# Layer norm of a cross-attention kernel: the scaling moved from ScalarE to VectorE one step later, gamma and beta to GpSimd

## The chip, the cores and the metric

The kernel runs on 1 core of one Trainium2 chip. The metric is the device time of one execution in microseconds (us); lower is better. The engines are TensorE (PE, with its weight loads PEld), VectorE (DVE), ScalarE (ACT), GpSimd (POOL) and SyncE (SP), which here only issues DMAs.

## The reference

16 batches of 256 query rows attend to 77 context rows, 16 heads of width 16, model width 256, all float32:

```python
Q, K, V = query @ Wq.T + bq, key_value @ Wk.T + bk, key_value @ Wv.T + bv     # split into 16 heads
attn = softmax(Q @ K.T / sqrt(16))
x = (attn @ V) @ W_o.T + b_o + query
mu, var = mean(x), mean((x - mu) ** 2)                                         # over the 256 columns
out = (x - mu) / sqrt(var + 1e-5) * ln_gamma + ln_beta
```

## The kernel before, in words

Each engine has its own instruction stream, written out by hand, and waits on counting semaphores. After a setup (weights, keys and values of all batches) the work goes in steps `s` = 0 to 18, one batch a step, as a software pipeline. In step `s` the following goes on:

- scores, exponentials and the sums over the context for batch `s`, in five units `u` = 0 to 4 (`UNITS`). For each unit TensorE makes `ps_s`; ScalarE makes `p` and `p_h` from it (lines 785 and 786); GpSimd makes the rest, `p_l = p - p_h` (line 1150). ScalarE may start unit `u` only when GpSimd has done the `p_l` of unit `u - 2`, since `p32` has two buffers. TensorE's `weigh` takes `p_h` and `p_l`.
- the maxima of batch `s + 1`: eight products `max_scores(0)` to `(7)` in two banks `ps_d` on TensorE, and eight reductions `max_of(0)` to `(7)` on VectorE (line 967). Product `j` waits for reduction `j - 2`. ScalarE's `write_maxima` (lines 804 and 805) ends this.
- the output of batch `s - 1`: `denominators` and `normalize` on VectorE (lines 977, 985), `turn_context` on TensorE (line 604), `ctx_h` on ScalarE (line 793, in a step without a query projection behind the exponentials of unit 3), `ctx_l` on VectorE (line 861), `project_out` on TensorE.
- the layer norm of batch `s - 2`: `residual` (line 996), `statistics` (line 1000), `aggregate` (line 1006), and at the end of VectorE's step `centre` (line 1016), (y - mean) * gamma, 128x256 twice. On GpSimd, at the end of its step, `rs_v` and `rs_y` (lines 1165 and 1171), the reciprocal root.
- the store of batch `s - 3`: ScalarE multiplies by the root (line 825, 128x256 twice), GpSimd adds beta (line 1158, 128x512) behind `p_l` of unit 2, SP stores (line 391).

Every even step up to 12 also projects the queries of the next two batches (`project_q`, `query_hi`, `query_lo`), and their DMAs (`load_zero`, `load_twins`, `load_mix`) stand on SP behind the store of the same step, which waits for GpSimd. Every odd step up to 11 ends VectorE's part with `split_x` (`xT_l`, line 861, 128x1024, two SBUF inputs). So the pattern repeats every two steps, about 21.1 us. Below, "odd step" and "even step" are meant in this sense. The last step of VectorE (`s` = 17) does its whole norm in one go, with its end on line 1052. The order of VectorE's step is this list, shortened:

```python
when(S.maxima, (max_of, 2))
...
when(S.maxima, (max_of, 3))
when(S.norm, (statistics, 0))
...
when(S.maxima, (max_of, 4))
...
when(S.output and s < B, (context_lo_part, 0, 1))
when(S.norm, (centre, 0), (centre, 1))
if S.split_x:
```

Of the kernel before, what the change touches and what calls it, by code (L numbers as in the profile page):

```python
# [68 lines left out]
KSLOTS = 4  # L69
PSLOTS = 4  # L70
P32SLOTS = 2
MROWS = 32
WARM_PASSES = 18
LOW_TILES = 3
# [63 lines left out]
def cross_attention_kernel(nc, xT, x, cT, wqT, wkT, wvT, woT, bias_cols, bias_rows, ident,  # L138
                           minus_low, minus_high, out):
    ctx = ExitStack()  # L140
    with ctx:
# [51 lines left out]


        q_mix = [sb("q_mix0", [P, HALVES, 2, PAIR], F32R)]
        result = sb("result", [P, 2, QT, D], F32)
        sb("under_vparts", [P, B * H * VP * VW // 2 - HALVES * 2 * PAIR - 2 * QT * D], F32)
# [4 lines left out]
        ctx_h, ctx_l = sb("ctx_h", [P, HALVES, SQ], F32R), sb("ctx_l", [P, HALVES, SQ], F32R)  # L202
        x_rows = sb("x_rows", [P, 2, QT, D], F32)
        q_mix.append(sb("q_mix1", [P, HALVES, 2, PAIR], F32R))
        y = sb("y", [P, QT, D], F32)


        def bank(name, shape):
# [20 lines left out]
        st_out = [sem(f"st_out{n}") for n in range(2)]  # L229
        st_last = sem("st_last")  # L230

        cleared_k = [sem(f"cleared_k{n}") for n in range(2)]
# [61 lines left out]
        def _(sp):  # L294
# [73 lines left out]
            def step(S):  # L368
                s = S.first
                if S.load_x:  # L370
                    S.wait(sp, x_lo, 1, 4, by=2)
                    sp.dma_start(xT_raw[:], xT_v[:, :, bass.ds(S.lin(SQ, 4 * SQ), PAIR)]).then_inc(ld_xT, 16)
                if S.load_k:
                    if s == 2:
                        sp.wait_ge(k_lo, HALVES * GROUPS)
                    S.wait(sp, pe_s, UNITS, 0)
                    if s <= 4:
                        move_minus((s // 2 + 1) % 2)
                    load_k(S.lin(1, 2), (s // 2 + 1) % 2)
                if S.scores:  # L380
                    if s == 0:
                        sp.wait_ge(pe_v, V_TASKS)
                        sp.wait_ge(pe_bo, 1)
                    S.wait(sp, y_done, 1, -1)
                    sp.dma_start(x_rows[:, s % 2], S.batch(x_v, 0, 0)).then_inc(ld_x[s % 2], 16)
                if s == 0:
                    load_v(1)
                if S.store:
                    if s < LAST_STEP:
                        S.wait(sp, result_done, 1, -2)  # L390
                        sp.dma_start(S.batch(out_v, 3, 0), result[:, (s - 3) % 2]).then_inc(st_out[(s - 3) % 2], 16)
                    else:
                        for t in range(QT):
                            sp.wait_ge(finished, t + 1)
                            sp.dma_start(out_v[B - 1][:, t], result[:, (B - 1) % 2, t]).then_inc(st_last, 16)
# [12 lines left out]
            all_steps(step)  # L408
            sp.wait_ge(st_out[0], 16 * B // 2)
            sp.wait_ge(st_out[1], 16 * (B // 2 - 1))  # L410
            sp.wait_ge(st_last, 16 * QT)


# [285 lines left out]
        def _(act):  # L699
# [73 lines left out]
            def step(S):  # L773
# [34 lines left out]
                for u in range(UNITS):  # L808
# [6 lines left out]
                    if u < HALVES and S.project_q:  # L815
                        S.wait(act, pe_q, 1, 3 + u)
                        S.wait(act, pe_s, UNITS, 0)
                        query_hi(u, (s // 2 + 1) % 2)
                    if u == (2 if S.project_q else 1) and S.store and s < LAST_STEP:

                        S.wait(act, root_done, 1, -2)
                        S.wait(act, centred, QT, -2 * QT)
                        for t in range(QT):
                            r = result[:, (s - 3) % 2, t]
# [31 lines left out]
        def _(dve):  # L856
# [92 lines left out]
            def step(S, between={}):  # L949

                s = S.first
                last = s == B + 1
                own = int(last)
                stats, meanvar = stats_all[:, own], meanvar_all[:, own]
                y_s = x_rows[:, (B - 1) % 2] if last else y[:]
# [34 lines left out]
                def residual():  # L990

                    S.wait(dve, pe_o, 1, -1)
                    S.wait(dve, ld_x[s % 2], 8, -8 * (s % 2))
                    if not last:
                        S.wait(dve, centred, QT, -2 * QT)
# [11 lines left out]

                def centre(t):

                    o = s % 2  # L1010
                    if t == 0:
                        if s == 2:
                            dve.wait_ge(ld_v[1], 16 * NSEG)
                        S.wait(dve, var_done, QT, -QT)
                        S.wait(dve, st_out[o], 8, -16 - 8 * o)
# [20 lines left out]
                if last:  # L1036
# [8 lines left out]
                    dve.wait_ge(var_done, QT * B)  # L1045
                    centre(0)
                    centre(1)
                    dve.wait_ge(centred, QT * B)
                    dve.wait_ge(root_done, B)
                    for t in range(QT):  # L1050
                        r = result[:, (B - 1) % 2, t]
# [59 lines left out]
        def _(pool):  # L1111
# [30 lines left out]
            def step(S):  # L1142
                s = S.first
                for u in range(UNITS):
# [6 lines left out]
                                         ALU.subtract).then_inc(rest16, 1)  # L1151
                    if s == 0 and u in (2, 3):
                        value_low(V_TASKS - 4 + u)
                    if u == (2 if s < B - 1 else 4) and S.store and s < LAST_STEP:

                        r = result[:, (s - 3) % 2]
                        S.wait(pool, scaled, QT, -2 * QT)
                        g_.tensor_tensor(r, r, beta_sb.unsqueeze(1).broadcast_to([P, QT, D]),  # L1158
                                         ALU.add).then_inc(result_done, 1)

                if S.norm:
                    slot = s % 2
                    S.wait(pool, var_done, QT, -QT)
                    S.wait(pool, root_done, 1, -3)
                    g_.tensor_scalar(rs_v[:, slot], meanvar_all[:, int(s == B + 1), :, 1], LN_EPS, 1.0,
                                     ALU.add, ALU.mult).then_inc(eps_added, 1)
                    S.wait(pool, eps_added, 1, -1)
                    S.wait(pool, scaled, QT, -3 * QT)
# [37 lines left out]
```

## Time and profile before

| | |
|---|---|
| median of 3 runs | 213.75 us (213.46 to 214.18) |
| the profiled execution, its own time | 215.56 us |
| its span, first to last instruction | 213.5 us |
| PE, PEld busy | 192.7 us (90%), 173.8 us (81%) |
| DVE busy | 175.5 us (82%) |
| ACT busy | 173.4 us (81%) |
| POOL busy | 152.6 us (71%) |
| mean granted TensorE clock | 0.98 |

Busy time is the sum over an engine's instructions; matmuls overlap, so PE's is not PE at its peak. Four engines lie close together, and no share of busy time tells which one sets the pace of the loop. The chain of work that ended last (each instruction followed back to what released it) and the timeline tell that.

### The profile page before, as it was taken

The page shows a single profiled execution, that of the slowest core. Times are in us where ns is not written, and L with a number is a line of the kernel's source. Part 1 is how long each engine was busy: PE and PEld are TensorE (multiplying, and loading weights), DVE is VectorE, ACT ScalarE, POOL GpSimd, SP SyncE. Part 2 cuts the span into 40 slices and gives each one's busy share as a digit, 9 for nine tenths or more (in the row PEclk, how much of TensorE's full clock was granted, in tenths as well). Part 3 has the DMA queues.
Part 4 walks back from the last instruction along what each step waited for, and adds up shares of the span by engine and source line. Part 5 has one row for each costly group of instructions (what it writes and reads, how often), then busy time and mean ns, then how long its engine had stood idle before and what let it go on. Part 6 is the DMA issues. An engine that isn't in the chain of part 4 may idle for free.

```text
span 213.5 us, 5610 instructions
## 1 busy us (share of the span) xinstructions
PE 192.7 (90%) x2070; PEld 173.8 (81%) x2070; DVE 175.5 (82%) x391; ACT 173.4 (81%) x313; POOL 152.6 (71%) x148
## 2 busy tenths in 40 slices
PE   7898999979999989989998999999999999896830
PEld 4897999869899978977988798879788979795730
DVE  5879985657797898989898989898988997982694
ACT  4588789979888979998999899989998998889130
POOL 9976542596557766896689678867887788979653
PEclk9999999999999999999999999999999999999695
DMA  5945521403656964795479438943793188111112
GB/s 183 350 101 138 146 51 40 163 28 95 204 108 176 240 205 97 186 242 159 86 195 249 136 83 206 244 136 80 187 250 71 53 217 236 54 49 54 49 49 98
DMA packets 32978, 30.39 MB, mean 142 GB/s; under 512 B 11306, under 2 KB 27672, under 8 KB 32952
## 3 DMA queue, kind: packets, MB, share of 16 engines
q1 hardware_dynamic: 31720, 28.78, 51.3%
q10 hardware_dynamic: 1232, 1.26, 2.0%
q8 instruction: 16, 0.26, 0.5%
q14 instruction: 10, 0.08, 0.1%
HBM read 11.32 MB, written 4.19 MB: 73 GB/s over the span
## 4 chain that ended last, share of the span: by engine, by line
PE 29%; POOL 28%; issue 16%; SPq 10%; ACT 6%; DMA 5%; DVE 4%; POOLq 0%; ACTq 0%; DVEq 0%
POOL p_l L1150 18%; PE ps_x L417 14%; PE ps_acc L417 6%; PE ps_s L417 6%; POOL result L1158 5%; SPq L341 4%; POOL rs_y L1171 3%; ACT p_h L786 3%; PE ps_d L417 3%; SPq L302 3%; DMA q_mix<-q_high 3%; DMA w_raw<-in_wkT 2%; DVE result L1016 2%; SPq L319 1%; DVE xT_l L861 1%
## 5 line engine op out<-in xcount | busy, mean ns | idle before, releaser
L1150 POOL TENSOR_TENSOR p_l<-p,p_h 128x512 f16<-128x512 f32 x80 | 95.2, 1195 | 43.2 <-ACT p_h L786 42.3
L967 DVE TENSOR_REDUCE maxima<-ps_d 128x4 f32<-128x308 f32 x128 | 57.3, 466 | 11.2 <-PE ps_d L417 9.4
L785 ACT ACTIVATE p<-ps_s 128x512 f32<-128x512 f32 x80 | 47.5, 594 | 11.2 <-PE ps_s L417 7.1
L786 ACT ACTIVATE p_h<-ps_s 128x512 f16<-128x512 f32 x80 | 47.3, 591 | 0.0
L417 PE MATMUL ps_s<-q_low,kblk 128*128 128x256 f32 x144 | 38.5, 287 | 2.0 <-issue 1.0
L417 PE MATMUL ps_acc<-vblk,p_h 128*128 128x34 f16 (+1 forms) x640 | 32.6, 183 | 0.9 <-POOL p_l L1150 0.9
L417 PEld LDWEIGHTS ps_acc<-vblk,p_h 128*128 128x128 f16 x640 | 28.0, 97 | 5.6 <-issue 1.6
L417 PE MATMUL ps_acc<-vblk,p_l 128*128 128x34 f16 (+1 forms) x320 | 30.5, 182 | 0.0
L417 PEld LDWEIGHTS ps_s<-q_low,kblk 128*128 128x128 f32 x144 | 27.0, 188 | 3.6 <-issue 1.4
L1016 DVE SCALAR_TENSOR_TENSOR result<-y,meanvar,rows_sb 128x256 f32<-128x256 f32 x30 | 28.6, 991 | 0.0
L417 PE MATMUL ps_s<-q_mix,kblk 128*128 128x256 f32 x96 | 26.3, 281 | 0.0
L417 PEld LDWEIGHTS ps_acc<-vblk,p_l 128*128 128x128 f16 x320 | 25.6, 96 | 0.0
L417 PE MATMUL ps_d<-kblk,q_high 128*128 128x308 f32 x64 | 22.0, 349 | 2.7 <-DVE maxima L967 2.6
L417 PE MATMUL ps_s<-q_high,kblk 128*128 128x256 f32 x80 | 23.2, 313 | 0.0
L1158 POOL TENSOR_TENSOR result<-result,rows_sb 128x512 f32<-128x512 f32 x15 | 19.4, 1296 | 3.6 <-ACT result L825 3.6
L417 PE MATMUL ps_d<-kblk,q_low 128*128 128x308 f32 x64 | 20.2, 321 | 1.2 <-ACT q_high L746 0.6
L861 DVE TENSOR_TENSOR ctx_l<-ps_x,ctx_h 128x512 fp32r<-128x512 f32 (+1 forms) x16 | 10.8, 675 | 10.1 <-ACT ctx_h L793 10.1
L417 PE MATMUL ps_x<-wo_h,ctx_l 128*128 128x256 f32 x64 | 18.5, 290 | 0.0
L417 PE MATMUL ps_x<-wo_h,ctx_h 128*128 128x256 f32 x64 | 18.5, 288 | 0.0
L417 PE MATMUL ps_x<-wo_l,ctx_h 128*128 128x256 f32 x64 | 18.4, 288 | 0.0
L417 PEld LDWEIGHTS ps_s<-q_mix,kblk 128*128 128x128 f32 x96 | 18.1, 189 | 0.0
L417 PE MATMUL ps_s<-q_lo,kblk 128*128 128x256 f32 x64 | 18.0, 281 | 0.0
(110 smaller groups left out, 506.1 us busy)
## 6 DMA issues: line engine op xcount, KB each, us to landing
xT_raw<-in_xT SPq DMA_DIRECT2D x8, 512.0 KB, 3.8
x_rows<-in_x SPq DMA_DIRECT2D x16, 256.0 KB, 3.4
out_dram<-result SPq DMA_DIRECT2D x15, 256.0 KB, 2.2
q_mix<-q_lo SPq DMA_DIRECT2D x12, 256.0 KB, 4.7
kblk<-kT SPq DMA_DIRECT2D x64, 38.5 KB, 2.3
kblk<-kblk SPq DMA_DIRECT2D x6, 256.0 KB, 3.3
q_mix<-q_low SPq DMA_DIRECT2D x6, 256.0 KB, 4.4
q_mix<-q_high SPq DMA_DIRECT2D x6, 256.0 KB, 5.1
```

Of the source, the lines that this page charges most:

```text
L302: sp.dma_start(kblk[rows, 2 * slot:2 * slot + 2, :, :, SKV * h:SKV * (h + 1)].rearrange("p b f l k -> p (b f l) k").bitcast(F32), kT[rows, ...
L319: sp.dma_start(q_mix[slot][to, :, part].bitcast(F32), source[slot][rows].bitcast(F32)).then_inc(ld_mix[slot], 16)
L341: sp.dma_start(vblk[part][row:row + n, seg].rearrange("p b f v w -> p (b f v w)"), vparts[part][key:key + n, h].rearrange("p b f v w -> p ...
L417: return nc.tensor.matmul(o, w, m, start=start, stop=stop, skip_group_check=True)
L785: nc.scalar.activation(p32[:, n % P32SLOTS], ps_s[n % 2][:], ACT.Exp, scale=SCALE)
L786: nc.scalar.activation(p_h[:, n % PSLOTS], ps_s[n % 2][:], ACT.Exp, scale=SCALE).then_inc(exp16, 1)
L861: return v_.tensor_tensor(out_, whole, hi.bitcast(F32), ALU.subtract)
L967: v_.tensor_reduce(maxima[:, t, h0:h0 + DMAX_HEADS], ps_d[((DMAX + 1) * (s + 1) + j) % 2][:, 0:DMAX_HEADS * SKV] .rearrange("p (h k) -> p ...
L1016: v_.scalar_tensor_tensor(result[:, o, t], y_s[:, t], meanvar[:, t, 0:1], gamma_sb, ALU.subtract, ALU.mult).then_inc(centred, 1)
L1150: g_.tensor_tensor(p_l[:, n % PSLOTS], p32[:, n % P32SLOTS], p_h[:, n % PSLOTS], ALU.subtract).then_inc(rest16, 1)
L1158: g_.tensor_tensor(r, r, beta_sb.unsqueeze(1).broadcast_to([P, QT, D]), ALU.add).then_inc(result_done, 1)
L1171: g_.tensor_tensor(rs_y[:, slot], rs_v[:, slot], minus_half[:], ALU.pow).then_inc(root_done, 1)
```

## The change

For batches 0 to 13 (`DIRECT`), VectorE computes (y - mean) * root in one `tensor_scalar` with two per-partition scalars, in the step after the statistics, behind `max_of(3)` and ahead of `statistics`. GpSimd then multiplies by gamma behind `p_l` of unit 2, and adds beta behind the same unit in odd steps and behind unit 3 in even steps. ScalarE has no part in it. The store goes out one step later, when its result is already there. `y` and the statistics get two buffers and `result` three. Batches 14 and 15 go as before.

```diff
-        result = sb("result", [P, 2, QT, D], F32)
+        result = sb("result", [P, RSLOTS, QT, D], F32)
-        y = sb("y", [P, QT, D], F32)
+        y_all = sb("y", [P, 2, QT, D], F32)
@@ SP, step
-                    if s < LAST_STEP:
+                    if 0 <= s - 4 < DIRECT:
+                        S.wait(sp, result_done, 1, -3)
+                        sp.dma_start(S.batch(out_v, 4, 0), result[:, (s - 4) % RSLOTS]).then_inc(st_out[(s - 4) % RSLOTS], 16)
+                    if s - 3 == DIRECT:
                         S.wait(sp, result_done, 1, -2)
...
@@ ACT, step
-                    if u == (2 if S.project_q else 1) and S.store and s < LAST_STEP:
+                    if u == (2 if S.project_q else 1) and S.store and DIRECT <= s - 3 < B - 1:
...
@@ DVE, step
+                def normalized():
+                    b = s - 3
+                    if b == 0:
+                        dve.wait_ge(ld_v[1], 16 * NSEG)
+                    S.wait(dve, root_done, 1, -2)
+                    if b >= RSLOTS:
+                        dve.wait_ge(st_out[b % RSLOTS], 16 * (b // RSLOTS))
+                    for t in range(QT):
+                        v_.tensor_scalar(result[:, b % RSLOTS, t], y_all[:, b % 2, t], meanvar_all[:, b % 2, t, 0:1],
+                                         rs_y[:, b % 2, t:t + 1], ALU.subtract, ALU.mult).then_inc(scaled, 1)
...
                 when(S.maxima, (max_of, 3))
+                when(S.store and s - 3 < DIRECT, (normalized,))
                 when(S.norm, (statistics, 0))
...
-                when(S.norm, (centre, 0), (centre, 1))
+                when(s == B, (centre, 0), (centre, 1))
@@ POOL, step
-                    if u == (2 if s < B - 1 else 4) and S.store and s < LAST_STEP:
+                    r = result[:, (s - 3) % RSLOTS]
+                    if u == GAMMA_AT and S.store and s - 3 < DIRECT:
                         S.wait(pool, scaled, QT, -2 * QT)
+                        g_.tensor_tensor(r, r, gamma_sb.unsqueeze(1).broadcast_to([P, QT, D]), ALU.mult).then_inc(gamma_done, 1)
+                    if u == (GAMMA_AT + 1 - s % 2 if s - 3 < DIRECT else 4) and S.store and s < LAST_STEP:
+                        S.wait(pool, scaled, QT, -2 * QT)
+                        if s - 3 < DIRECT:
+                            S.wait(pool, gamma_done, 1, -2)
                         g_.tensor_tensor(r, r, beta_sb.unsqueeze(1).broadcast_to([P, QT, D]),
                                          ALU.add).then_inc(result_done, 1)
```

## Rows read from the trace of the kernel before

**Rows 1.** One pair of steps: window, length, busy PE, PEld, DVE, ACT, POOL, clock, DMA.
```profile
111.04:132.13 21.09, 20.08 (x234) 17.90 (x233) 19.14 (x44) 19.30 (x36) 16.21 (x18) 1.00 0.66 167
```

**Rows 2.** The chain that ended last, 126 to 141 us: start, us, what.
```profile
126.48 1.25 POOL result L1158
127.73 1.31 POOL p_l L1150
129.04 0.84 issue
...
131.45 0.71 POOL rs_y L1171
132.16 2.26 POOL p_l L1150 x2
...
137.14 1.39 DVE result L1016
138.53 1.15 DVE xT_l L861
139.72 1.66 PE ps_x L417 x6
```

**Rows 3.** Timeline of VectorE in the same odd step.
```profile
132.22 0.74 DVE L1000 BATCH_NORM_STATS2 stats<-y 128x6 f32<-128x256 f32 x2
...
133.03 0.44 DVE L967 TENSOR_REDUCE maxima<-ps_d 128x4 f32<-128x308 f32 x1
...
136.70 1.83 DVE L1016 SCALAR_TENSOR_TENSOR result<-y,meanvar,rows_sb 128x256 f32<-128x256 f32 x2
```

**Rows 4.** Timeline of TensorE there: product 6 of the maxima, last score of unit 3.
```profile
133.53 0.41 PE L417 MATMUL ps_d<-kblk,q_high 128*128 128x308 f32 x1 [0.43 <-DVE maxima L967]
...
134.01 0.28 PE L417 MATMUL ps_s<-q_low,kblk 128*128 128x256 f32 x1
```

**Rows 5.** Timeline of ScalarE there: exponentials of unit 3.
```profile
134.49 0.60 ACT L785 ACTIVATE p<-ps_s 128x512 f32<-128x512 f32 x1
```

**Rows 6.** Timeline of GpSimd there: units 0 to 2, and unit 3.
```profile
132.12 3.57 POOL L1150 TENSOR_TENSOR p_l<-p,p_h 128x512 f16<-128x512 f32 x3
...
136.90 1.35 POOL L1150 TENSOR_TENSOR p_l<-p,p_h 128x512 f16<-128x512 f32 x1
```

**Rows 7.** Timeline of VectorE in the even step that follows.
```profile
144.56 0.26 DVE L977 RECIPROCAL recip<-ps_acc 128x16 f32<-128x16 f32 x1 [0.63 <-PE ps_acc L417]
```

**Rows 8.** By line: min/median/max ns of one centring and one `p_l`.
```profile
L1016 DVE SCALAR_TENSOR_TENSOR result<-y,meanvar,rows_sb x30: 472/981/1475, 62.6 to 205.7; 128x256 f32<-128x256 f32 x30
L1150 POOL TENSOR_TENSOR p_l<-p,p_h x80: 1155/1167/1362, 36.2 to 197.9; 128x512 f16<-128x512 f32 x80
```

**Rows 9.** Groups of instructions: busy us, mean ns of one, idle before.
```profile
L1158 POOL TENSOR_TENSOR result<-result,rows_sb 128x512 f32<-128x512 f32 x15 | 19.4, 1296 | 3.6 <-ACT result L825 3.6
L825 ACT ACTIVATE result<-result,rs_y 128x256 f32<-128x256 f32 x30 | 13.6, 507 | 2.6 <-POOL rs_y L1171 2.6
L1093 DVE CAST bo_parts<-rows_sb 128x256 fp32r<-128x256 f32 x1 | 0.3, 297 | 0.0
```

**Rows 10.** Timeline of VectorE in the setup: two casts.
```profile
16.80 1.69 DVE L922 CAST kblk<-vblk 32x768 fp32r<-32x768 f32 x1
18.51 1.24 DVE L923 CAST kblk<-vblk 32x464 fp32r<-32x464 f32 x1
```

**Rows 11.** Timeline of GpSimd in the setup, beside them.
```profile
16.27 1.80 POOL L1134 MEMSET vblk<- 128x2040 uint32 x1
18.19 1.31 POOL L1125 TENSOR_TENSOR vparts<-vwhole,vparts 77x512 f16<-77x512 f32 x1
```

**Rows 12.** Waits in SP's queue: who for whom, us in total, times, longest.
```profile
SPq L391 <- POOL result L1158: 45.8, 15, 9.0
```

**Rows 13.** Waits of the compute engines, 44 to 90 us.
```profile
PE ps_s L417 <- DMA q_mix<-q_high: 0.7, 1, 0.7
```

**Rows 14.** Timeline of GpSimd in step 16: beta of batch 13.
```profile
204.19 1.28 POOL L1158 TENSOR_TENSOR result<-result,rows_sb 128x512 f32<-128x512 f32 x1 [2.62 <-ACT result L825]
```

More of the change, by code:

```diff
@@ L71 @@
 P32SLOTS = 2
+RSLOTS = 3
+GAMMA_AT = 2
+DIRECT = B - 2
 MROWS = 32
@@ L195, in cross_attention_kernel @@
         q_mix = [sb("q_mix0", [P, HALVES, 2, PAIR], F32R)]
-        result = sb("result", [P, 2, QT, D], F32)
-        sb("under_vparts", [P, B * H * VP * VW // 2 - HALVES * 2 * PAIR - 2 * QT * D], F32)
+        result = sb("result", [P, RSLOTS, QT, D], F32)
+        sb("under_vparts", [P, max(1, B * H * VP * VW // 2 - HALVES * 2 * PAIR - RSLOTS * QT * D)], F32)
         p32 = sb("p32", [P, P32SLOTS, 2, SQ], F32)
@@ L228, in cross_attention_kernel @@
         ld_x = [sem(f"ld_x{n}") for n in range(2)]
-        st_out = [sem(f"st_out{n}") for n in range(2)]
+        st_out = [sem(f"st_out{n}") for n in range(RSLOTS)]
+        gamma_done = sem("gamma_done")
         st_last = sem("st_last")
@@ L388, in step @@
                 if S.store:
-                    if s < LAST_STEP:
+                    if 0 <= s - 4 < DIRECT:
+                        S.wait(sp, result_done, 1, -3)
+                        sp.dma_start(S.batch(out_v, 4, 0), result[:, (s - 4) % RSLOTS]).then_inc(st_out[(s - 4) % RSLOTS], 16)
+                    if s - 3 == DIRECT:
                         S.wait(sp, result_done, 1, -2)
-                        sp.dma_start(S.batch(out_v, 3, 0), result[:, (s - 3) % 2]).then_inc(st_out[(s - 3) % 2], 16)
-                    else:
+                        sp.dma_start(S.batch(out_v, 3, 0), result[:, (s - 3) % RSLOTS]).then_inc(st_out[(s - 3) % RSLOTS], 16)
+                    if s == LAST_STEP:
                         for t in range(QT):
                             sp.wait_ge(finished, t + 1)
-                            sp.dma_start(out_v[B - 1][:, t], result[:, (B - 1) % 2, t]).then_inc(st_last, 16)
+                            sp.dma_start(out_v[B - 1][:, t], result[:, (B - 1) % RSLOTS, t]).then_inc(st_last, 16)
                 if S.project_q and s >= 2:
@@ L408, in _ @@
             all_steps(step)
-            sp.wait_ge(st_out[0], 16 * B // 2)
-            sp.wait_ge(st_out[1], 16 * (B // 2 - 1))
+            for n in range(RSLOTS):
+                sp.wait_ge(st_out[n], 16 * len(range(n, B - 1, RSLOTS)))
             sp.wait_ge(st_last, 16 * QT)
@@ L818, in step @@
                         query_hi(u, (s // 2 + 1) % 2)
-                    if u == (2 if S.project_q else 1) and S.store and s < LAST_STEP:
+                    if u == (2 if S.project_q else 1) and S.store and DIRECT <= s - 3 < B - 1:
                         S.wait(act, root_done, 1, -2)
-                        S.wait(act, centred, QT, -2 * QT)
+                        act.wait_ge(centred, QT)
                         for t in range(QT):
-                            r = result[:, (s - 3) % 2, t]
+                            r = result[:, (s - 3) % RSLOTS, t]
                             nc.scalar.activation(r, r, copy, scale=rs_y[:, (s - 3) % 2, t:t + 1]).then_inc(scaled, 1)
@@ L952, in step @@
                 last = s == B + 1
-                own = int(last)
+                own = s % 2
                 stats, meanvar = stats_all[:, own], meanvar_all[:, own]
-                y_s = x_rows[:, (B - 1) % 2] if last else y[:]
+                y_s = x_rows[:, (B - 1) % 2] if last else y_all[:, own]
                 def accumulated(f):
@@ L994, in residual @@
                     if not last:
-                        S.wait(dve, centred, QT, -2 * QT)
+                        S.wait(dve, scaled, QT, -3 * QT)
                     v_.tensor_tensor(y_s.rearrange("p t d -> p (t d)"), ps_x[1][:],
@@ L1008, in centre @@
                 def centre(t):
-                    o = s % 2
+                    o = (s - 2) % RSLOTS
                     if t == 0:
-                        if s == 2:
-                            dve.wait_ge(ld_v[1], 16 * NSEG)
                         S.wait(dve, var_done, QT, -QT)
-                        S.wait(dve, st_out[o], 8, -16 - 8 * o)
+                        dve.wait_ge(st_out[o], 16 * ((s - 2) // RSLOTS))
                     v_.scalar_tensor_tensor(result[:, o, t], y_s[:, t], meanvar[:, t, 0:1], gamma_sb,
                                             ALU.subtract, ALU.mult).then_inc(centred, 1)
+                def normalized():
[8 more added lines that the diff above has]
+                                         rs_y[:, b % 2, t:t + 1], ALU.subtract, ALU.mult).then_inc(scaled, 1)
                 def context_lo_part(*halves):
@@ L1047, in step @@
                     centre(1)
-                    dve.wait_ge(centred, QT * B)
+                    dve.wait_ge(centred, 2 * QT)
                     dve.wait_ge(root_done, B)
                     for t in range(QT):
-                        r = result[:, (B - 1) % 2, t]
+                        r = result[:, (B - 1) % RSLOTS, t]
                         v_.scalar_tensor_tensor(r, r, rs_y[:, (B - 1) % 2, t:t + 1], beta_sb, ALU.mult, ALU.add).then_inc(finished, 1)
@@ L1164, in step @@
                     S.wait(pool, root_done, 1, -3)
-                    g_.tensor_scalar(rs_v[:, slot], meanvar_all[:, int(s == B + 1), :, 1], LN_EPS, 1.0,
+                    g_.tensor_scalar(rs_v[:, slot], meanvar_all[:, slot, :, 1], LN_EPS, 1.0,
                                      ALU.add, ALU.mult).then_inc(eps_added, 1)
```

1 line of the change is left out of this document (removed).

## The prediction

> **What bounds the kernel now.** I read the windows of one pair of steps first, then the chain that ended last, then each engine's timeline around it. The windows [rows 1] show a pair of 21.09 us in which VectorE works 19.14, ScalarE 19.30 and GpSimd 16.21, at a granted clock of 1.00 (its full 2.4 GHz). No engine is full, so the pace is set by a ring of waits. The reader is to see in the chain [rows 2] that it goes through GpSimd from unit 2 of the even step (whose `p_l` ends at 126.48) to unit 1 of the odd one, with one gap of 0.84 us, then through ScalarE's exponentials and `ctx_h`, through `ctx_l` and the two centrings on VectorE, `xT_l`, and TensorE's query projection.
>
> The chain hides how close VectorE is behind it. In the odd step VectorE's `max_of(4)` starts at 133.03 [rows 3]; TensorE's product 6 starts at 133.53 and stood idle 0.43 us for it; the last score of unit 3 comes behind that product, at 134.01 for 0.28, so it ends at 134.29 [rows 4]. ScalarE starts the exponentials of unit 3 at 134.49 [rows 5], which waited for `p_l` of unit 1, done at 134.42 (132.16 + 2.26) [rows 2]. So the middle of VectorE's odd step has some 0.2 us of slack, no more. What is put ahead of `max_of(4)` beyond that delays unit 3, then `ctx_h`, which stands behind unit 3 on ScalarE, then `ctx_l`, `project_out` and the next step. In the even step there is more: VectorE waits 0.63 us for TensorE just ahead of `max_of(4)` [rows 7].
>
> **Where VectorE and GpSimd get in each other's way.** One centring takes 472 ns at best, 981 in the median and 1475 at worst [rows 8]. The pair at 136.70 shows why: it lasts 1.83 us, beside beta until about 136.9 and `p_l` of unit 3, which starts at 136.90 and takes 1.35 in place of 1.17 [rows 3, 6, 8]. The first centring gets through as beta ends and holds up `p_l` by 0.18; the second waits until `p_l` ends at 138.25 and is itself over at 138.53. A centring reads two tensors, but a cast, which reads one, does the same: the cast of 768 elements from 16.80 ends at 18.49, 0.42 after GpSimd's memset (18.07); that of 464 elements from 18.51 ends at 19.75, 0.25 after GpSimd's subtraction (19.50) [rows 10, 11]. Undisturbed a cast of 256 elements takes 297 ns [rows 9]. The two waiting casts differ by 0.17 us for 304 elements, so one of 256 would end about 0.25 - 208 x 0.17 / 304 = 0.13 us after GpSimd lets it in.
>
> **The change part by part.**
>
> Removed from VectorE: the pair of centrings, 2 x 0.98 us a step [rows 8]. In odd steps it is on the chain, ahead of `xT_l`. But TensorE is only just behind there: its projection starts at 139.72 as `xT_l` ends at 139.68 (138.53 + 1.15) [rows 2], and it works 20.08 of 21.09 us [rows 1]; that is worth at most 0.3 us a pair by TensorE's idle share, and I take nothing, since `ctx_l` and `project_out` remain.
>
> Removed from ScalarE: 2 x 0.51 us a step [rows 9]. In the odd step ScalarE waits for GpSimd anyway. In the even step it would let unit 4 come earlier and close GpSimd's gap of 0.84 us [rows 2], but GpSimd fills it itself:
>
> Added to GpSimd: gamma, an operation of beta's form, 1.25 us on the chain [rows 2] (1.30 at most [rows 9]). In the even step: from 126.48, gamma 1.25, `p_l` of unit 3 in 1.17 (its 1.31 less the wait for a centring), beta 1.25: unit 4 starts at 130.15, where it was 129.88 (129.04 + 0.84). That is 0.25 us later, and all that follows up to unit 1 of the odd step with it. In the odd step gamma and beta stand between units 2 and 3, where the next reader of a unit is the following step; GpSimd has 4.88 us idle a pair (21.09 - 16.21) [rows 1] against 2.5 added, so I cost it at nothing. Were that cover gone it would be 1.25 us a pair.
>
> Added to VectorE's middle: two `tensor_scalar` of 256 elements. The trace has none of this size. From below: as the cast, 0.30 us each, overlapping like their neighbours to 0.45 for two [rows 9]. From above, if each waits for a whole `p_l` of 1.17: 2 x (1.17 + 0.13) = 2.6. I take waiting, since the row nearest to it in form, the cast, waits. In the odd step VectorE comes to the pair at 132.22, GpSimd starts unit 0 at 132.12 and works without a gap to 135.65 [rows 3, 6]. And the pair must itself wait for `rs_y`, which ended at 132.16 and will end at 132.41, when GpSimd's next `p_l` is ready to go. Two outcomes:
> - GpSimd goes first: both wait. Unit 0 ends at 132.12 + 0.25 + 1.17 = 133.54, the first is over 0.13 later, unit 1 takes until 134.85, the second is over at about 134.95. Statistics and `max_of(4)` come 2.7 us late (134.95 - 132.22); less the slack of 0.2 the step is 2.5 us longer.
> - VectorE goes first: only the second waits, until 133.75. 1.5 late, 1.3 us longer.
>
> The Trainium skill, "SBUF — State Buffer", section "Who interferes with whom", says that a VectorE instruction in a 2-port mode, with `tensor_scalar` named among them, and a GpSimd instruction exclude each other for a whole instruction. The casts agree (0.42 and 0.25 us after GpSimd's end); no row shows it for `tensor_scalar`.
>
> In the even step the pair finds GpSimd in the gap between units 0 and 1 once the odd step has grown, and its 0.5 us fit into the 0.63 idle [rows 7]: nothing.
>
> Moved store: SP issues it one step later, when its result is there. SP's 45.8 us of waits for GpSimd go [rows 12], and the six DMAs of even steps behind them start sooner. A compute engine waited for these once, 0.7 us [rows 13]: a gain of 0.7 at most, at step 4, taken as nothing since the longer step 3 covers that wait.
>
> The end: in step 16 beta (1.28) starts at 204.19 upon ScalarE's pair [rows 14]; now gamma comes ahead of it, 1.28 more, less some 0.3 by which VectorE's pair is shorter than ScalarE's (1.01 against 0.5 to 0.7). All that follows is one series through GpSimd: +1.0 us. Step 14, without a query projection, meets the same row of `p_l`, partly covered: +0.7 (0.4). Step 15 reduces no maxima: nothing.
>
> **The sum**, over odd steps 5 to 13 (five), step 3 with its 0.7 us of waiting for a DMA and a later start on GpSimd, step 14, and the end. Both wait: 5 x 2.5 + 0.8 + 0.7 + 1.0 = 15.0. One waits: 5 x 1.3 + 0.5 + 0.4 + 1.0 = 8.4. The profiled execution took 215.56 us (span 213.5 and 2.06 around it), 0.8% over the median of the runs, 213.75. To that median the two give 215.56 + 15.0 = 230.6, x 213.75 / 215.56 = 228.6, and 222.1. Who goes first hangs on less than 0.1 us, which the trace doesn't settle; I take the middle, 225.5.
>
> **The rivals.**
> - No waiting (218 us). `tensor_scalar` takes turns with nothing, like the statistics. For it: the two statistics take 0.74 us together beside `p_l` and aren't stretched [rows 3, 6]. Against it: the casts. The pair then costs 0.25 for the later `rs_y` and 0.6 for itself, less 0.2 of slack: 5 x 0.65 + 0.4 + 1.0 = 4.6 us, 218.3. The Trainium skill (same page and section) has this rule too: one SBUF input outside the 2-port modes doesn't contend.
> - GpSimd alone (216 us). VectorE's time is won back elsewhere in the step and only 0.25 a pair and the end remain: 6 x 0.25 + 1.0 = 2.5.
> - Faster (212 us). The pair runs in no more than the 0.2 us of slack beyond what it frees, and from there the lost centrings decide: TensorE's projection comes up to 0.3 us earlier in six pairs, and the DMA wait of 0.7 goes: -2.5, +1.0 at the end: about -1.5. For it: VectorE loses 1.96 us a step and ScalarE 1.01. Against it: they are lost at the end of the step, and the new work stands ahead of `max_of(4)`, for which TensorE waits already.
>
> **How the numbers follow.** Waiting 0.68, no waiting 0.14, GpSimd alone 0.06 (half a per cent and more over before), faster 0.08, and 0.04 for gains and losses that cancel. A measurement tells about 0.3% from no change. Faster 0.09, same 0.05, slower 0.86. The time is that of the waiting pair, 225.5, its own range 221 to 230; down to 217 the range takes in no waiting: 217 to 230.5.
>
> **What would show it.** `tensor_scalar` well above 0.3 us in odd steps (1.2 to 1.4 for the waiting one) and near 0.3 in even steps; `p_l` of units 0 and 1 stretched by about 0.1; product 6 waiting 1.5 to 3 us for `max_of(4)` in odd steps; a pair of 22.4 to 23.6 us; idle time of GpSimd moved ahead of unit 3 of odd steps; SP no longer waiting for GpSimd. The prediction is wrong if `tensor_scalar` takes 0.3 to 0.4 us beside `p_l`, or if product 6 waits no longer than before.

## The result: 235.7 us, 9.8% slower

The changed kernel takes 235.66 us (median of 6 runs, 233.86 to 236.47) against 214.03 (213.46 to 215.33) for the kernel before in the same job: a ratio of 1.098, with a 95% interval of 1.095 to 1.102. The forecast was 225.5, with a range of 217 to 230.5: the direction was right, the size was not. The profiled execution took 236.47 us with a span of 234.7, so 21.2 us more than the span before.

**The pair of steps.** The windows of after, one pair of steps (it answers to [rows 1]) and the stretch behind TensorE's wait in its odd step (length, busy PE, PEld, DVE, ACT, POOL, clock, DMA):

```profile
138.20:162.11 23.91, 20.93 (x234) 19.06 (x234) 18.68 (x44) 17.78 (x32) 18.24 (x19) 0.93 0.58 150
141.90:146.30 4.40, 4.39 (x53) 4.23 (x54) 2.96 (x8) 2.83 (x5) 3.50 (x3) 0.64 0.11 34
```

The pair has grown from 21.09 to 23.91 us, by 2.8. VectorE and ScalarE do less work in it than before (18.68 and 17.78 against 19.14 and 19.30). GpSimd does more, and TensorE is busy for longer (20.93 against 20.08) with the same 234 matmuls, part of them at a lower clock. And the granted clock of a pair, 1.00 before, is 0.93: over the 4.4 us behind product 6 it is 0.64, a mean between the two levels of 1.2 and 2.4 GHz.

The odd step on VectorE (it answers to [rows 3]), and the pair in the even step that follows:

```profile
138.32 2.36 DVE L1033 TENSOR_SCALAR result<-y,meanvar,rs_y 128x256 f32<-128x256 f32 x2
140.60 0.74 DVE L1007 BATCH_NORM_STATS2 stats<-y 128x6 f32<-128x256 f32 x2
141.26 0.23 DVE L984 RECIPROCAL recip<-ps_acc 128x16 f32<-128x16 f32 x1
141.42 0.43 DVE L974 TENSOR_REDUCE maxima<-ps_d 128x4 f32<-128x308 f32 x1
...
151.28 0.95 DVE L1033 TENSOR_SCALAR result<-y,meanvar,rs_y 128x256 f32<-128x256 f32 x2
```

GpSimd beside it (it answers to [rows 6]):

```profile
137.53 0.70 POOL L1193 TENSOR_TENSOR rs_y<-rs_v,minus_half 128x2 f32<-128x2 f32 x1
138.20 3.56 POOL L1168 TENSOR_TENSOR p_l<-p,p_h 128x512 f16<-128x512 f32 x3
141.72 1.27 POOL L1175 TENSOR_TENSOR result<-result,rows_sb 128x512 f32<-128x512 f32 x1
...
150.59 1.17 POOL L1168 TENSOR_TENSOR p_l<-p,p_h 128x512 f16<-128x512 f32 x1
```

The last line is unit 0 of the even step. In the kernel before, the same one is this:

```profile
141.72 1.17 POOL L1150 TENSOR_TENSOR p_l<-p,p_h 128x512 f16<-128x512 f32 x1
```

From unit 0 to unit 0, the odd step has grown from 9.60 us (141.72 - 132.12) to 12.39 (150.59 - 138.20). The even step has not: 11.52 us (162.11 - 150.59) against 11.50 (153.22 - 141.72). So the whole loss of a pair of steps arises in its odd step.

The pair of `tensor_scalar` begins 0.12 us behind GpSimd's unit 0 and lasts as long as two `p_l`. GpSimd's three `p_l` take 3.56 us, as before (3.57): it loses nothing, VectorE does all the waiting. `max_of(4)` comes 3.22 us behind unit 0 (141.42 - 138.20) instead of 0.91 (133.03 - 132.12).

By line, one of the new instructions on VectorE, min/median/max ns:

```profile
L1033 DVE TENSOR_SCALAR result<-y,meanvar,rs_y x28: 400/976/1256, 68.2 to 223.3; 128x256 f32<-128x256 f32 x28
```

The shortest, 400 ns, is the undisturbed one (in run 6 below, where GpSimd stands still beside most of them, the median is 406); the longest is that plus most of a `p_l`.

TensorE's product 6 and the scores behind it, at the lower clock (it answers to [rows 4]: 0.43 us of idle time, 0.41 for the product, 0.28 for a score):

```profile
141.91 0.62 PE L424 MATMUL ps_d<-kblk,q_high 128*128 128x308 f32 x1 [2.72 <-DVE maxima L974]
142.33 0.41 PE L424 MATMUL ps_s<-q_low,kblk 128*128 128x256 f32 x1
```

ScalarE's exponentials of unit 3 (to [rows 5]) now wait for TensorE:

```profile
143.21 0.60 ACT L792 ACTIVATE p<-ps_s 128x512 f32<-128x512 f32 x1 [2.67 <-PE ps_s L424]
```

**The clock.** The page's row of TensorE's granted clock in 40 slices, after:

```profile
PEclk9999999999999999799979997999799979896785
```

A slice is 5.9 us. The five 7s ahead of the last six slices are the odd steps 5 to 13. Before, the row holds nothing below 9 until the last three slices. Here the clock fell behind an idle stretch of TensorE of 2.7 us; behind the 0.43 us of before it did not.

**SP.** Waits in its queue, after (to [rows 12]: 45.8 us, 15 times):

```profile
SPq L395 <- POOL result L1180: 16.4, 2, 9.4
```

Both waits are behind 186 us: the stores no longer wait inside the loop, as the change means them to. TensorE had waited once, for 0.7 us, for a DMA behind them [rows 13], so there was next to nothing to win; run 7 below shows no gain.

**Where the 21.2 us of span arise.** By the starts of GpSimd's unit 0 in both kernels: up to step 13, +11.7 (186.00 against 174.31); step 13, +3.6 (12.38 us for 8.77); step 14, +2.7 (12.23 for 9.56); step 15 to the end, +3.2 (24.1 for 20.9). The last three together are 9.5 us, nearly half of the loss, behind the start of step 13.

### The profile page after: what moved, and what is told of

Its sections match the earlier page's. It is cut to its first block, busy times and chain, and to the rows that moved or that the text cites. A ratio compares the mean times of both kernels' runs of the same rounds, so it can differ in the third digit from the quotient of the medians.

```text
span 234.7 us, 5596 instructions
## 1 busy us (share of the span) xinstructions
PE 197.2 (84%) x2070; PEld 179.4 (76%) x2070; DVE 175.0 (75%) x391; ACT 162.8 (69%) x285; POOL 169.2 (72%) x162
## 4 chain that ended last, share of the span: by engine, by line
PE 39%; POOL 20%; DVE 17%; issue 12%; SPq 7%; ACT 2%; DMA 1%; POOLq 0%; DVEq 0%; ACTq 0%
PE ps_x L424 14%; PE ps_s L424 8%; PE ps_acc L424 8%; POOL p_l L1168 6%; DVE result L1033 5%; PE ps_d L424 5%; DVE maxima L974 5%; SPq L345 4%; PE ps_x L611 3%; POOL vparts L1143 3%; DVE stats L1007 3%; SPq L306 2%; POOL result L1175 2%; POOL kblk L1133 2%; POOL result L1180 2%
## 5 line engine op out<-in xcount | busy, mean ns | idle before, releaser
L1168 POOL TENSOR_TENSOR p_l<-p,p_h 128x512 f16<-128x512 f32 x80 | 93.1, 1169 | 48.3 <-ACT p_h L793 47.5
L424 PE MATMUL ps_s<-q_low,kblk 128*128 128x256 f32 x144 | 39.2, 291 | 1.4 <-issue 1.2
L424 PE MATMUL ps_d<-kblk,q_high 128*128 128x308 f32 x64 | 24.4, 386 | 18.3 <-DVE maxima L974 17.8
L424 PE MATMUL ps_acc<-vblk,p_h 128*128 128x34 f16 (+1 forms) x640 | 34.3, 187 | 0.3 <-issue 0.3
L424 PEld LDWEIGHTS ps_acc<-vblk,p_h 128*128 128x128 f16 x640 | 29.9, 100 | 5.1 <-issue 1.8
L424 PE MATMUL ps_acc<-vblk,p_l 128*128 128x34 f16 (+1 forms) x320 | 31.9, 186 | 0.0
L424 PEld LDWEIGHTS ps_s<-q_low,kblk 128*128 128x128 f32 x144 | 28.5, 198 | 2.0 <-issue 1.3
L424 PEld LDWEIGHTS ps_d<-kblk,q_high 128*128 128x128 f32 x64 | 13.2, 209 | 20.8 <-DVE maxima L974 20.8
L424 PEld LDWEIGHTS ps_acc<-vblk,p_l 128*128 128x128 f16 x320 | 27.0, 99 | 0.0
L1033 DVE TENSOR_SCALAR result<-y,meanvar,rs_y 128x256 f32<-128x256 f32 x28 | 23.3, 872 | 1.8 <-POOL rs_y L1193 1.8
L424 PE MATMUL ps_s<-q_high,kblk 128*128 128x256 f32 x80 | 24.1, 323 | 0.0
L1180 POOL TENSOR_TENSOR result<-result,rows_sb 128x512 f32<-128x512 f32 x15 | 19.6, 1304 | 2.2 <-ACT result L832 1.0
L1175 POOL TENSOR_TENSOR result<-result,rows_sb 128x512 f32<-128x512 f32 x14 | 17.9, 1278 | 2.9 <-DVE result L1033 2.9
```

Of the source, the lines that this page charges most:

```text
L424: return nc.tensor.matmul(o, w, m, start=start, stop=stop, skip_group_check=True)
L1033: v_.tensor_scalar(result[:, b % RSLOTS, t], y_all[:, b % 2, t], meanvar_all[:, b % 2, t, 0:1], rs_y[:, b % 2, t:t + 1], ALU.subtract, ALU ...
L1168: g_.tensor_tensor(p_l[:, n % PSLOTS], p32[:, n % P32SLOTS], p_h[:, n % PSLOTS], ALU.subtract).then_inc(rest16, 1)
L1175: g_.tensor_tensor(r, r, gamma_sb.unsqueeze(1).broadcast_to([P, QT, D]), ALU.mult).then_inc(gamma_done, 1)
```

## The experiments

The theory: two `tensor_scalar` in the middle of VectorE's odd step wait for two whole `p_l`; TensorE's product 6 waits for them; TensorE's clock then falls. The rivals put the loss down to gamma on GpSimd, to the place of the pair, or to the end of the kernel.

**1. The pair on its own.** The kernel before, with two more `tensor_scalar` into a scratch tile behind `max_of(3)`, and nothing else of the change.

```diff
+                def extra():
+                    S.wait(dve, root_done, 1, -2)
+                    for t in range(QT):
+                        v_.tensor_scalar(scratch[:, t], gamma_sb, meanvar_all[:, 0, t, 0:1],
+                                         rs_y[:, (s - 3) % 2, t:t + 1], ALU.subtract, ALU.mult)
...
                 when(S.maxima, (max_of, 3))
+                when(S.store and s - 3 < B - 2, (extra,))
```

> The kernel before, with nothing but two tensor_scalar of 128x256 added (gamma's row into a tile that nobody reads) behind max_of(3), in the steps and after the wait of the change. Theory (the pair at this place is the cost): the pair takes 2.2 to 2.5 us in odd steps, the clock falls behind it, 230 to 238 us. Rival (the costs come from gamma on GpSimd, the store or the buffers): 214 to 218 us.

Measured: 236.07 us (ratio 1.100, 1.093 to 1.107). The pair in an odd step on VectorE:

```profile
139.69 2.23 DVE L1023 TENSOR_SCALAR scratch<-rows_sb,meanvar,rs_y 128x256 f32<-128x256 f32 x2
```

TensorE's product 6 behind it:

```profile
143.15 0.62 PE L418 MATMUL ps_d<-kblk,q_high 128*128 128x308 f32 x1 [2.59 <-DVE maxima L968]
```

These two instructions a step cost as much as the whole change, with centrings, ScalarE, gamma, beta and stores all as before. That is enough to make the loss.

**2. One instruction instead of two.** The same, with `for t in range(1)`.

> The kernel before with one added tensor_scalar behind max_of(3) instead of two (two took 236.1 us). Theory (each waits for one whole p_l): it takes 1.1 to 1.2 us in odd steps, max_of(4) is some 1.1 us late and the kernel takes 220 to 225 us. Rival (the wait comes once for the pair, whatever their number): 230 us or more.

Measured: 217.43 us (1.012, 1.008 to 1.017), and cheaper than either text expected. One pair of steps, windows:

```profile
132.66:154.28 21.62, 19.79 (x233) 17.92 (x233) 20.30 (x46) 19.27 (x36) 15.99 (x17) 1.00 0.66 161
```

Its odd step on VectorE:

```profile
132.84 1.14 DVE L1023 TENSOR_SCALAR scratch<-rows_sb,meanvar,rs_y 128x256 f32<-128x256 f32 x1
...
137.62 0.69 DVE L862 TENSOR_TENSOR ctx_l<-ps_x,ctx_h 128x512 fp32r<-128x512 f32 x1 [0.55 <-ACT ctx_h L794]
138.23 1.05 DVE L1017 SCALAR_TENSOR_TENSOR result<-y,meanvar,rows_sb 128x256 f32<-128x256 f32 x2
139.21 1.22 DVE L862 TENSOR_TENSOR xT_l<-xT_raw,xT_h 128x1024 fp32r<-128x1024 f32 x1
```

TensorE there:

```profile
135.21 0.41 PE L418 MATMUL ps_d<-kblk,q_high 128*128 128x308 f32 x1 [1.50 <-DVE maxima L968]
```

GpSimd there:

```profile
137.44 1.16 POOL L1158 TENSOR_TENSOR p_l<-p,p_h 128x512 f16<-128x512 f32 x1
```

`ctx_l` and `xT_l` of the kernel before, to compare:

```profile
136.09 0.69 DVE L861 TENSOR_TENSOR ctx_l<-ps_x,ctx_h 128x512 fp32r<-128x512 f32 x1 [0.71 <-ACT ctx_h L793]
...
138.45 1.21 DVE L861 TENSOR_TENSOR xT_l<-xT_raw,xT_h 128x1024 fp32r<-128x1024 f32 x1
```

The `tensor_scalar` does wait for one `p_l`, and product 6 comes 1.07 us later (1.50 - 0.43). But the pair of steps is only 0.53 us longer, and the clock stays at 1.00. Counted from unit 0 (132.66 here, 132.12 before), `ctx_l` starts 0.99 later (4.96 us against 3.97) and `xT_l` only 0.22 (6.55 against 6.33). The `p_l` of unit 3 has not moved: it starts 4.78 us behind unit 0 in both (137.44 - 132.66, and 136.90 - 132.12 [rows 6]). The centrings, 0.99 later, now meet only its last 0.37 us, and take 1.05 us in place of the 1.83 of [rows 3]. So the first wait costs about 3 us in all and the second nearly 19. Waiting time does not add up in a straight line here.

**3. TensorE kept busy in its wait.** The changed kernel, with 16 matmuls that nobody reads ahead of product 6, in the steps without a query projection.

```diff
+                        if j == 6 and s >= 3 and not S.project_q:
+                            S.wait(pe, ctx_lo, 1, -1)
+                            for _ in range(16):
+                                mm(ps_x[0][:, 0:SQ], warm_rows[:, 0:P], warm_rows[:], True, True)
                         S.wait(pe, max_done, DMAX, DMAX + j - 1)
```

> The changed kernel, with 16 matmuls on zeros (about 1.8 us) on TensorE ahead of product 6 in steps without a query projection, where it waits 2.7 us; their output is overwritten unread. Theory (the fall of the clock after the wait is part of the cost, about 0.8 us in a pair): clock 0.97 or more, 229 to 232 us. Rival (the clock costs nothing, it falls where TensorE waits anyway): 235 us as without them.

Measured: 230.03 us (1.075, 1.068 to 1.082), inside the theory's 229 to 232. TensorE, odd step:

```profile
137.40 1.92 PE L424 MATMUL ps_x<-warm_rows 128*128 128x256 bf16 x16
140.09 0.41 PE L424 MATMUL ps_d<-kblk,q_high 128*128 128x308 f32 x1 [0.78 <-DVE maxima L978]
```

One pair of steps, windows:

```profile
136.41:159.39 22.98, 21.58 (x252) 19.38 (x249) 18.89 (x44) 17.73 (x32) 18.28 (x20) 1.00 0.58 151
```

Product 6 comes as late as before the filling (1.92 + 0.78 = 2.70), but now runs in 0.41 us, and the clock is 1.00. The pair is 22.98 us, 0.93 less than after. So of the 2.8 us a pair some 1.9 is waiting and 0.9 is clock. Over the kernel the clock is 5.6 us by the medians (235.66 - 230.03), 7.1 by the two profiled spans.

**4. A form of the instruction that does not wait.** The changed kernel, its `tensor_scalar` also writing out an accumulator, its place unchanged.

```diff
-                                         rs_y[:, b % 2, t:t + 1], ALU.subtract, ALU.mult).then_inc(scaled, 1)
+                                         rs_y[:, b % 2, t:t + 1], ALU.subtract, ALU.mult, accum_out=acc_sb[:, t:t + 1]).then_inc(scaled, 1)
```

> The changed kernel, with an accumulator output on the two tensor_scalar, at the same place; the output need not be the layer norm. If only a form that can use a second port waits for GpSimd, this one takes 0.40 to 0.50 us each at any time, and the kernel takes 217 to 221 us. If every VectorE instruction on SBUF of this kind waits, 2.3 us for the pair in odd steps and 235 us remain.

Measured: 220.8 us (1.031, 1.025 to 1.036), in the theory's range. The line's two instructions, min/median/max ns:

```profile
L1034 DVE TENSOR_SCALAR_CACHE_REDUCE result<-y,meanvar,rs_y x28: 527/530/537, 68.4 to 208.0; 128x256 f32<-128x256 f32 x28
L1034 DVE DVE_READ_ACCUMULATOR result<-y,meanvar,rs_y x28: 77/81/85, 68.8 to 208.5; 128x1 f32 x28
```

All 28 take the same 530 ns, in odd and even steps, beside the same three `p_l`: slower by itself than the 400 ns of the plain form, yet 15 us cheaper. (With the accumulator the output is no longer the layer norm, so this version is a measurement and not a remedy.) The Trainium skill, "SBUF — State Buffer", section "Who interferes with whom", names `tensor_scalar` among the operations that can hold the port pair that VectorE and GpSimd share, and excepts the form that writes out its accumulator. This run agrees: 530 ns at every meeting, against up to 1256.

What is left, 6.7 us over the kernel before, is of the size of run 2: the two instructions and their reads of the accumulator still take about 1.1 us ahead of `max_of(4)`, product 6 waits 1.36 us for it, and a pair of steps takes 21.61 us (155.25 - 133.64, by unit 0), 0.52 over before. Of the 6.1 us of span, 2.6 arise up to step 13 and 3.5 behind it.

**5. Gamma left out.** The changed kernel without the multiplication by gamma on GpSimd (and without the wait for it in front of beta).

```diff
-                        g_.tensor_tensor(r, r, gamma_sb.unsqueeze(1).broadcast_to([P, QT, D]), ALU.mult).then_inc(gamma_done, 1)
+                        pass
```

> The changed kernel without GpSimd's multiplication by gamma, which is left out. Theory: 232 to 235 us, since GpSimd has room in the longer pair and only the end of the kernel gains about 1.3 us. Rival (GpSimd's load is what costs): 217 to 222 us.

Measured: 234.67 us (1.096, 1.090 to 1.102). That is 1.0 us below the changed kernel, which lies within the two intervals: in this order of the work gamma costs next to nothing. The prediction had priced it at 2.5 us in all.

**6. The pair late in odd steps.** The changed kernel, with the pair ahead of `ctx_l` in odd steps and in step 14, and behind `max_of(3)` in even steps as it was.

```diff
-                when(S.store and s - 3 < DIRECT, (normalized,))
+                late = s % 2 == 1 or s == B - 2
+                when(S.store and s - 3 < DIRECT and not late, (normalized,))
...
+                when(S.store and s - 3 < DIRECT and late, (normalized,))
                 when(S.output and s < B, (context_lo_part, 0, 1))
```

> The changed kernel, with VectorE's pair of tensor_scalar moved from behind max_of(3) to ahead of ctx_l in odd steps and in step 14. There GpSimd has to wait for the pair, so nothing holds it up. Theory (the pair waits for two p_l ahead of max_of(4), and TensorE's wait lets its clock fall): the pair takes 0.5 to 1.2 us there, product 6 waits no longer than before, the clock is back at 0.97 or more, 216 to 219 us. Rival (GpSimd's added gamma is what costs): 230 us or more.

Measured: 235.02 us (1.098, 1.090 to 1.105). The theory's 216 to 219 missed by 16 us. VectorE, from the pair of an odd step to that of the next, even step:

```profile
144.57 0.73 DVE L1033 TENSOR_SCALAR result<-y,meanvar,rs_y 128x256 f32<-128x256 f32 x2
...
146.14 1.60 DVE L868 TENSOR_TENSOR xT_l<-xT_raw,xT_h 128x1024 fp32r<-128x1024 f32 x1 [0.25 <-ACT xT_h L756]
...
152.24 2.55 DVE L1033 TENSOR_SCALAR result<-y,meanvar,rs_y 128x256 f32<-128x256 f32 x2 [1.01 <-POOL rs_y L1195]
```

GpSimd beside it:

```profile
145.38 1.29 POOL L1177 TENSOR_TENSOR result<-result,rows_sb 128x512 f32<-128x512 f32 x1 [0.68 <-DVE result L1033]
146.81 2.08 POOL L1182 TENSOR_TENSOR result<-result,rows_sb 128x512 f32<-128x512 f32 x1
148.85 2.29 POOL L1170 TENSOR_TENSOR p_l<-p,p_h 128x512 f16<-128x512 f32 x2
...
151.50 0.70 POOL L1195 TENSOR_TENSOR rs_y<-rs_v,minus_half 128x2 f32<-128x2 f32 x1
152.17 2.47 POOL L1170 TENSOR_TENSOR p_l<-p,p_h 128x512 f16<-128x512 f32 x2
```

The odd step is cured: the pair takes 0.73, because GpSimd stands still, waiting for it. But gamma then starts late, beta meets `xT_l` and takes 2.08 in place of 1.28, and the reciprocal root comes only at 152.2. The pair of the even step waits 1.01 us for it, starts as GpSimd starts the next two `p_l`, and waits for both (2.55 us). The same loss has moved one step on: product 6 of even steps now waits 2.8 us.

**7. The same without gamma.** Run 6 with gamma left out as in run 5.

> The kernel with the pair late in odd steps and in step 14 only (the one that took 235 us), without GpSimd's multiplication by gamma, which is left out. Theory (there GpSimd, with gamma, beta and the wait for the pair in a row, makes rs_y late, so that the pair of the even step waits for rs_y and then for two p_l): without gamma rs_y is 1.3 us earlier, the pair of even steps takes 1.3 us or less, 217 to 222 us. Rival (the even step loses by its place alone): 230 us or more.

Measured: 214.47 us (0.9997, 0.996 to 1.003), the time of the kernel before, and better than the expectation. Gamma is worth 20.6 us between runs 6 and 7 and 1.0 us between the changed kernel and run 5: what an operation costs depends on whether the root behind it is awaited. In run 7 the pair of the even step waits for no root and takes 1.43 us (the theory said 1.3 or less). The run also shows that all the rest of the change together (the pair in a good place, ScalarE's and the centrings' work gone, the store a step later, the buffers) comes to nothing that can be told from the noise; it does not show that each part does.

**8. The pair late in every step up to 15.** Run 6 with `late = s < B`, gamma kept.

> The changed kernel with the pair of tensor_scalar ahead of ctx_l in every step up to 15, even steps too. Theory (what costs is VectorE waiting for p_l ahead of max_of(4), in whichever step the pair stands there): product 6 waits 0.5 us at most in both steps, the clock is 0.97 or more, 217 to 222 us, with 0.3 to 0.5 us lost per even step where the pair delays ctx_l. Rival (GpSimd can't carry gamma as well, wherever the pair stands): 228 us or more.

Measured: 222.4 us (1.037, 1.031 to 1.042), just above the theory's range, and the best time of any version that does the whole change and computes the layer norm. One pair of steps, windows:

```profile
134.13:156.07 21.94, 20.21 (x234) 17.97 (x233) 17.93 (x45) 17.48 (x32) 19.05 (x19) 1.00 0.63 157
```

TensorE's product 6 in the odd step:

```profile
135.09 0.41 PE L424 MATMUL ps_d<-kblk,q_high 128*128 128x308 f32 x1 [0.27 <-DVE maxima L974]
```

The clock is full, and product 6 waits only 0.27 us in the odd step and 0.22 in the even one. GpSimd is busy 19.05 of 21.94 us and waits 0.55 us for the pair in each step. That this is what costs the remaining 8 us was not tested.

**9. Centrings behind `xT_l`.** The kernel before, with only the order of these two on VectorE swapped in odd steps, to see what taking the centrings off that place is worth.

```diff
-                when(S.norm, (centre, 0), (centre, 1))
                 if S.split_x:
                     S.wait(dve, x_hi, 1, 5, by=2)
                     split_x()
+                when(S.norm, (centre, 0), (centre, 1))
```

> The kernel before, with VectorE's xT_l ahead of the two centrings in odd steps instead of behind them. Theory (the centrings are on the chain, but TensorE is less than 0.3 us behind): xT_l ends 1 to 1.8 us earlier and 0 to 0.3 us a pair is gained, 212.0 to 214.2 us. Rival (xT_l now holds up a p_l of GpSimd): 214.5 to 217 us.

Measured: 217.19 us (1.011, 1.007 to 1.016): a loss. VectorE in the odd step:

```profile
116.28 2.11 DVE L861 TENSOR_TENSOR xT_l<-xT_raw,xT_h 128x1024 fp32r<-128x1024 f32 x1 [0.25 <-ACT xT_h L749]
118.32 1.81 DVE L1016 SCALAR_TENSOR_TENSOR result<-y,meanvar,rows_sb 128x256 f32<-128x256 f32 x2
```

GpSimd beside it, units 3 and 4:

```profile
116.13 1.18 POOL L1150 TENSOR_TENSOR p_l<-p,p_h 128x512 f16<-128x512 f32 x1
118.67 1.17 POOL L1150 TENSOR_TENSOR p_l<-p,p_h 128x512 f16<-128x512 f32 x1 [1.36 <-ACT p_h L786]
```

`xT_l` takes up the wait for `p_l` of unit 3 in the centrings' stead (2.11 for 1.15). The centrings still follow, and meet the `p_l` of unit 4 (1.81).

**10. The end.** Three versions of the changed kernel, in which the new way ends with batch 9, 11 and 12 (`DIRECT` smaller, the old way for the rest).

```diff
-DIRECT = B - 2
+DIRECT = B - 6
...
-                when(s == B, (centre, 0), (centre, 1))
+                when(S.norm and s - 2 >= DIRECT, (centre, 0), (centre, 1))
```

(`B - 4` and `B - 3` in the other two.)

> The changed kernel with the new way for batches 0 to 9 only, and 10 to 15 in the old way (centring, ScalarE, beta), so that steps 13 to 16 have no pair behind max_of(3). If the end of the kernel costs what the two traces show (6 to 7 us from step 13 on): 228 to 231 us. If it costs 1.7 to 2.5 us as forecast: 233 to 235 us.

> The changed kernel with the new way for batches 0 to 11 only; 12 to 15 go the old way, so steps 15 and 16 have no pair and no gamma. Theory (step 15 costs too: its pair waits beside the three p_l like the others, the only chain of the end goes through it, and TensorE's clock falls further behind it; step 16 adds 1.0): by the traces step 15 to the end took 24.1 us against 20.9 before, so about 232.5 us (231.5 to 233.3). Rival (the forecast's step: step 15 nothing, the end 1.0): 234.6, no different from the version that goes the new way up to batch 12.

> The changed kernel with the new way for batches 0 to 12, so only step 16 has no pair and no gamma. Theory and the forecast agree here: gamma ahead of beta in the last series through GpSimd costs about 1.0 us, so 234.6 us (234.2 to 235.0). Rival (step 16 is worth nothing or far more, since the idle stretches of the end move with the clock): 235.6, or below 233.5.

Measured: 227.19 us (1.058, 1.050 to 1.065), 232.86 (1.087, 1.081 to 1.092) and 234.84 (1.098, 1.091 to 1.104). Windows of the first, from unit 0 of step 13 to the end:

```profile
186.73:225.60 38.87, 26.41 (x323) 23.71 (x321) 27.69 (x67) 22.72 (x46) 28.64 (x31) 0.89 0.26 80
```

That stretch is 39.2 us in the kernel before (213.5 - 174.31) and 48.7 after (234.7 - 186.00), so with the old way (38.9) it is as before. Steps 13 to 16 cost 8.5 us of the 21.6, a little more than the theory's 228 to 231 allowed. Taken apart by the medians: step 16 costs 0.8 (235.66 - 234.84), step 15 2.0 (234.84 - 232.86), steps 13 and 14 the other 5.7. The versions ran in different jobs; by their ratios to the kernel before, times 214.03, the three are 0.2, 2.3 and 6.2. The intervals of the last two versions overlap a little, so the cost of step 15 is right in sign and rough in size, and that of step 16 lies within the noise. Why step 15 costs something, VectorE after, in step 15:

```profile
210.74 2.34 DVE L1033 TENSOR_SCALAR result<-y,meanvar,rs_y 128x256 f32<-128x256 f32 x2 [1.79 <-POOL rs_y L1193]
213.00 0.74 DVE L1007 BATCH_NORM_STATS2 stats<-y 128x6 f32<-128x256 f32 x2
...
213.94 0.48 DVE L992 SCALAR_TENSOR_TENSOR ctx_n<-ps_acc,v_unscale,recip 128x256 f32<-128x256 f32 x1
```

The chain that ended last, after, at the same place:

```profile
211.84 1.24 DVE result L1033
213.08 0.66 DVE stats L1007 x2
...
214.02 0.41 DVE ctx_n L992
...
214.47 1.11 PE ps_x L611 x4
```

`ctx_n` of the same step in the kernel before, where unit 0 starts at 192.64:

```profile
192.47 0.48 DVE L985 SCALAR_TENSOR_TENSOR ctx_n<-ps_acc,v_unscale,recip 128x256 f32<-128x256 f32 x1
```

No maxima are reduced in step 15, but `ctx_n` stands behind the pair on VectorE too, and TensorE's `turn_context` behind that. The pair first waits 1.79 us for the root and then for two `p_l`, so `ctx_n` starts 3.33 us behind unit 0 (213.94 - 210.61), where it started 0.17 ahead of it before. `turn_context` then runs at the lower clock (1.11 us for four, at 0.50; 0.60 at the full one in an odd step of run 3). Before, the chain ran through GpSimd here and VectorE had room.

## Why the prediction was wrong, step by step

- **What bounds the kernel; the slack ahead of `max_of(4)`.** Right. The loss came through `max_of(4)`, product 6 and unit 3, as put. Lateness is not passed on in full, though: 1.07 us at product 6 cost 0.53 a pair in run 2.
- **`tensor_scalar` waits for `p_l`.** Right: 976 ns in the median, 400 at least; the "no waiting" rival fell in runs 1 and 4. The lower bound read off the cast, 0.30 us, was too low: 0.40. "`p_l` stretched by 0.1" did not come: 3.56 us for three.
- **Who goes first: the middle of two outcomes.** This step failed first. The prediction said that the order hangs on less than 0.1 us, which the trace does not settle, and took the mean of 228.6 and 222.1. GpSimd goes first in each of the odd steps 5 to 13, as at 138.20 and 138.32 above. Rows 3 and 6 already had the order, 132.12 and 132.22. The prediction made a tie of it, by leaving VectorE's arrival at 132.22 and letting both engines wait for a root that comes 0.25 us later. In the trace after, VectorE waits for no root: it goes from `max_of(3)` to the pair without idle time and is 0.12 us behind GpSimd (0.30 in step 5), where it was 0.10 before. The likeliest outcome was "both wait". A mean of two outcomes is a time that neither gives.
- **"Both wait", 2.5 us an odd step.** Up to step 13 this came out as 10.8, and measured 11.7, but for mixed reasons. The waiting alone is 1.9 a pair (run 3), less than the 2.5; TensorE's clock adds 0.9, which no term of the sum held. Had only the order been right, 228.6 would have stood near run 3's 230.0, the time with the clock held for most of the kernel; but that nearness would be luck. In run 3 the loss is 8.1 us up to step 13 and 6.0 behind it (in spans), where "both wait" has 10.8 and 4.2: one term too dear, the other too cheap. The term that was missing altogether, the clock, is 5.6 us.
- **The even step: nothing.** Right for the change: 11.52 us against 11.50. The pair does not quite fit the gap, though. It starts at 151.28, beside the `p_l` of unit 0 (until 151.76), and takes 0.95 us. Wrong as a general rule: in run 6 it is the even step that pays.
- **Gamma on GpSimd: 0.25 a pair, +1.0 at the end.** Too dear, if anything: 1.0 us in all by run 5, and 0.2 to 0.8 for step 16 by the last version of run 10, both within the noise. The warning beside it, what it costs if its cover goes, was too low: 20.6 us between runs 6 and 7, not 1.25 a pair.
- **The end: step 14 0.7, step 15 nothing.** This failed too. Step 13, priced as one more odd step at 2.5, is 3.6 longer (2.3 with the clock held). Step 14 is 2.7 longer, and 1.5 with the clock held (run 3: 11.08 for 9.56); the cover it was granted, "partly covered", was a guess. Step 15 costs 2.0 to 2.3. It was costed by the one reader, `max_of(4)`, that is missing there, and not by who else stands behind the pair on VectorE.
- **Removed work on VectorE and ScalarE, and the store: nothing.** Right: run 7 has all of it, and the time of the kernel before. Run 9 shows why for the centrings: what they cost is largely the meeting with `p_l`, and the next instruction takes that over.

The sum as it should have been, in spans: 11.7 up to step 13, 3.6, 2.7 and 3.2. Of it, 7.1 is clock by the two profiled spans (that of after is of the slowest of its six executions), and 5.6 by the medians. What stays open: run 3's filling leaves step 15 and the end without a filled wait, so the clock's whole share there was not separated; why 0.3 of the 0.53 us of run 2 arises behind `xT_l` was not followed; and what costs the last 8 us of run 8 is argued, not shown.

## What to carry to other kernels

Before an operation is put into a gap, look not only at how busy its engine is but at what the neighbour that shares its access does at that moment: two instructions of 400 ns took 2.4 us here beside GpSimd and 0.7 where GpSimd itself was waiting for it. When two outcomes hang on a small difference, take one, by the order that the rows already show, and give the other its chance. And when a wait of TensorE grows from tenths of a microsecond to some 2.7 us, price the clock behind it as well: here it was another half of the waiting.

## What the runs showed of the hardware that was not expected

- TensorE's granted clock fell, to a mean of 0.64 over the next 4.4 us, behind the idle stretch of 2.72 us. It need not have fallen by the first matmul: behind stretches of 2.59 (run 1) and 2.82 us (run 6) that took 0.62 us, but behind another of 2.83 us in run 6, and one of 2.45 in step 14 of the changed kernel, it took the 0.41 of the full clock, and the clock was near 0.50 only about 1 us later. Behind one of 1.50 us in run 2, and one of 0.78 behind filling in run 3, it stayed at 1.00.
- A `tensor_scalar` of 256 float32 columns with two per-partition scalars takes 400 ns undisturbed, where the cast of the same size took 297 [rows 9]. Beside `p_l` it took up to 1256 ns in the changed kernel. The form with an accumulator takes 530 ns, and 81 more for the read of the accumulator; none of its 28 took over 537.
- GpSimd is held up too when it comes second: beta (1.28 us) took 2.08 beside `xT_l`, which reads two tensors (run 6).
